# Path pass of a four-layer graph kernel: another order of gathers and scatters on GpSimd

## The reference, cut to what matters

```
f0 = x0 @ W_l10 * na * INV_SQRT_MUL            # features of every node
f1 = einsum('num,uv->nvm', x1, W_l11) * na3 * INV_SQRT_MUL
h  = silu(edge_len_emb @ W_mlp1 / 4);  w = h @ W_mlp2 / 8      # weights of every edge
g0, g1 = f0[i], f1[i]                          # gather at the edge's source
m0a = w0 * g0 * sh0
m0b = w3 * (g1 * sh1).sum(-1) * INV_SQRT3
m1a = w1 * g0 * sh1;  m1b = w2 * g1 * sh0
n   = segment_sum([m0a, m0b, m1a, m1b], j) / sqrt(16)          # sum at the destination
out = ...n @ W_l2...;  alpha = (n0a @ A0 + n0b @ A1) * na * INV_SQRT_2MUL
x   = layernorm(x + sc + alpha * out)
```

## Time and profile before

| what | us |
|---|---|
| median of three timed executions | 5012.12 (5004.49 to 5012.53) |
| the profiled execution's own time | 5035.27 |
| its span, first to last instruction | 5033.5 |
| path pass on POOL, first gather to end of last scatter | 4471.9 to 5025.0 |
| POOL busy over the span | 2801.2 (56%) |
| PE, DVE, ACT busy over the span | 3759.1, 3757.5, 3210.8 |

### The profile page before, as it was taken

How to read it: one execution, slowest core, us unless ns; L and a number is a source line. 1 busy time by engine, 2 the same in 40 slices (tenths; PEclk the granted TensorE clock), 3 DMA queues, 4 the chain that set the end, 5 groups by cost and what they waited for, 6 DMA issues and landing times. The chain is left out here.

```text
span 5033.5 us, 104447 instructions
## 1 busy us (share of the span) xinstructions
PE 3759.1 (75%) x23663; PEld 3111.3 (62%) x23663; DVE 3757.5 (75%) x10843; ACT 3210.8 (64%) x11475; POOL 2801.2 (56%) x2759
## 2 busy tenths in 40 slices
PE   6355889966786677767776878878698997967775
PEld 5254778855556554745575555556587886856664
DVE  1576789978878886978696877879687786747665
ACT  2022779967887686868685543358698795646554
POOL 0473767711760375047302767767476776757776
PEclk9699999978998798979876767779899998978777
DMA  8899999955885597568665446657599896862221
GB/s 180 111 289 284 358 371 317 284 151 157 265 271 153 164 295 247 148 193 278 226 181 150 151 150 184 202 171 240 192 344 327 293 354 223 246 140 61 64 69 52
DMA packets 918273, 1074.23 MB, mean 213 GB/s; under 512 B 202779, under 2 KB 565065, under 8 KB 917106
## 3 DMA queue, kind: packets, MB, share of 16 engines
q1 hardware_dynamic: 763570, 890.24, 54.1%
q0 software_dynamic: 90944, 180.06, 14.1%
q10 hardware_dynamic: 63556, 1.81, 1.8%
HBM read 509.54 MB, written 566.14 MB: 214 GB/s over the span
## 5 line engine op out<-in xcount | busy, mean ns | idle before, releaser
L2366 POOL DMA_INDIRECT H<-gat_rows,src_i x784 | 801.1, 1022 | 876.0 <-POOLq L80 638.0
L1917 POOL DMA_INDIRECT s_G<-sage_rows,src_i x588 | 595.3, 1012 | 286.4 <-issue 175.9
L1696 POOL DMA_INDIRECT r_G<-rel_rows,idx x392 | 404.6, 1032 | 165.9 <-issue 116.7
L2555 PE MATMUL p_M<-Wg,p_hT 128*128 128x132 f32 x2352 | 342.3, 290 | 59.3 <-DVE p_res L2612 45.3
L2555 PEld LDWEIGHTS p_M<-Wg,p_hT 128*128 128x128 f32 x2352 | 296.8, 196 | 106.6 <-issue 91.4
L2612 DVE SCALAR_TENSOR_TENSOR p_res<-p_M,p_rr,cg 128x132 f32<-128x132 f32 x1176 | 333.8, 346 | 2.7 <-PE p_M L2555 1.7
L2694 PEld LDWEIGHTS p_pl_p<-Wn,p_pl_h 128*128 128x128 f32 x1568 | 204.1, 197 | 205.4 <-ACT p_pl_h L2788 158.5
L1305 PE MATMUL d_S<-ones,d_sqT 128*128 128x1 f32 x1568 | 227.6, 266 | 135.6 <-DVE d_ve L1450 135.6
L1709 PE MATMUL r_t<-r_oh,relv 8*128 8x512 f32 x294 | 203.9, 779 | 166.1 <-DMA r_G<-rel_rows,idx 79.0
L2694 PE MATMUL p_pl_p<-Wn,p_pl_h 128*128 128x128 f32 x1568 | 223.3, 287 | 136.2 <-ACT p_pl_h L2788 136.2
L1305 PEld LDWEIGHTS d_S<-ones,d_sqT 128*128 128x128 f32 x1568 | 221.9, 218 | 162.4 <-issue 128.9
(11 more groups left out here) (483 smaller groups left out, 12423.8 us busy)
## 6 DMA issues: line engine op xcount, KB each, us to landing
gat_rows<-p_res SPq DMA_DIRECT2D x294, 264.0 KB
sage_rows<-p_pl_s SPq DMA_DIRECT2D x294, 256.0 KB
gat_rows<-x_row SPq DMA_DIRECT2D x98, 536.0 KB
gat_rows<-d_res SPq DMA_DIRECT2D x147, 264.0 KB
d_hs<-gat_rows SPq DMA_DIRECT2D x147, 256.0 KB
s_hT<-sage_slots_t SPq DMA_DIRECT2D x147, 256.0 KB
slot_rows<-H SPq DMA_DIRECT2D x49, 544.0 KB, 11.4
x_x<-in_x SPq DMA_DIRECT2D x98, 256.0 KB
```

Source lines behind the costliest of these rows:

```text
L1696: pool.indirect_dma_start(self.G[:, g % 4, k, :], None, table, bass.IndirectOffsetOnAxis(index[:, c:c + 1], 0), bounds_check=bound, oob_is ...
L1917: pool.indirect_dma_start(self.G[:, g % 4, k, :], None, kn.st[self.l], bass.IndirectOffsetOnAxis(kn.idx[:, c:c + 1], 0), bounds_check=boun ...
L2366: pool.indirect_dma_start(kn.H[:, c, 0:width], None, table, bass.IndirectOffsetOnAxis(index[:, c:c + 1], 0), bounds_check=bound, oob_is_er ...
L2555: mm = pe.matmul(self.pM[self.bank(b, j)][:, k // 2, (k % 2) * TW:(k % 2 + 1) * TW], self.hT[l][:, b.s2, k * P:(k + 1) * P], kn.Wg[:, l, : ...
```

## The change: what it does

It replaces the fixed distance of 12 groups by a formula. After the gathers of group g, all scatter groups up to `due` are issued, where `due = max(g + 1 - 15, 0) * 41 // 34`. Scatter groups are issued in the same order as before and with the same waits; gathers too. Written out, scatter group 0 follows the gathers of group 15, then one scatter group follows each gather group, except that two follow those of groups 19, 24, 29, 34, 39, 44 and 48, and eight are left for the end.

```
-        LATE = 12
+        FIRST, LAST = 15, 8
...
+        put = 0
         for g in range(kn.KG):
             if g >= 2:
                 pool.wait_ge(self.gin[(g - 2) % 4], ((g - 2) // 4 + 1) * 16 * KT)
...
-            if g >= LATE:
-                place(g - LATE)
-        for g in range(kn.KG - LATE, kn.KG):
-            place(g)
+            due = max(g + 1 - FIRST, 0) * (kn.KG - LAST) // (kn.KG - FIRST)
+            for n in range(put, due):
+                place(n)
+            put = max(put, due)
+        for n in range(put, kn.KG):
+            place(n)
```

## The result

The changed kernel took 4982.29 us (median of 5 timed executions, 4978.33 to 4990.09) against 5004.49 for the kernel before (5 executions, 5000.35 to 5012.53). The ratio is 0.9955, 95% interval 0.9941 to 0.9969: about 22 us faster. The forecast was 4992 us and, against the starting median of 5012.12, 0.9960. The ratio came as forecast; the absolute time is 9.7 us under the forecast and 0.7 us under the stated range.

The account below looks back on a forecast made before the run. POOL's gathers and scatters bound the path pass, except at six waits for VectorE. 7.4 us at the head, 0 in the middle and 13.7 less some 1 at the end make 20 us off 5012.12: 4992 us, range 4983 to 5007.

Parts of the forecast that it names:

- Level: Whole kernel: 20 us taken off the timed median of 5012.12, itself 23 us under the profiled execution, gives 4992 us.
- 21.1 us is all that any reordering can win: Path pass: POOL's six waits for VectorE, 22.9 us less 0.30 ordinary gap each, cap the gain at 21.1 us.
- Head: Start of path pass: three more gather groups before scatter 0 remove POOL's 7.72 us wait, winning 7.4 us.
- Middle: Middle of path pass: compute keeps up with a scatter group every 9.9 us instead of 10.9; term zero.
- 1 us of cover at the tightest: Middle, after a doubled scatter: results come at T + 26.0 at worst, wanted at T + 27.
- End: End of path pass: compute is 22 us ahead, so 13.7 us of POOL waits go, less some 1 us.
- 1 to 4 given as a sign: Path pass: POOL's wait for VectorE falls from 22.9 us to 1 to 4, all ahead of scatters 42 to 44.
- (a): Last steps: TensorE at low clock, a 12.17 us step between norms 42 and 43; 15 us won, 4997; chance 0.19.
- (b): Path pass: longer POOL instructions, stops at doubles and end waits leave 9 us won, 5003, nothing measurable; chance 0.17.
- (c): Middle: compute becomes the bound, period rises over 9.9 us and the kernel is slower, 5028 at 10.8; chance 0.06.
- about 7.3 us of work: Middle: compute's period of 10.9 us held 3.6 us of waiting, leaving about 7.3 us of work per group.
- (d): Head: sixteen gather groups come first instead of fifteen; the sum is the same, no chance of its own.

Follow-up runs that it names:

- the edit to the dots: Changed kernel's VectorE reduction of the dots written as two additions; POOL durations 420.4 to 407.7 us, from e_pick_act to e_both.
- the head's half alone: Against the changed kernel, sixteen gather groups first but one scatter group behind each, no doubled scatters; ratio 1.0006 to the kernel before, pass 564.5 us.
- e_far: Against the changed kernel, twenty-five gather groups go ahead of the first scatter instead of sixteen, same end; ratio 0.9957 to the kernel before, pass 537.7 us.
- e_pick_act: Changed kernel with the copy of the edge records moved from VectorE to ScalarE; ratio 0.9951 to the kernel before, pass 542.6 us.
- e_both: Changed kernel with the record copy on ScalarE and the dots' reduction as two additions; ratio 0.9933 to the kernel before, pass 530.7 us.
- e_two_adds: Changed kernel with only the dots' reduction written as two VectorE additions; ratio 0.9932 to the kernel before, pass 533.4 us.

## Why the prediction was right in its steps and wrong in its time

- **Level, the step that failed: "The timed median of 5012.12 is 23 us under that execution; taken off it, 20 us give 4992 us".** That median was the middle of three executions. With two more it was 5004.49, and over the jobs of this study the same kernel had medians of 5004.49, 5012.59, 5009.17, 5016.8 and 5011.73; the changed one 4982.29, 4992.75 and 4993.46. Two of the last three are within 1.5 us of 4992. The gain was about right: 22.2, 19.8 and 18.3 us between the medians of the three pairs, against 20. Of the 9.7 us by which the forecast missed, 7.6 are the starting level and 2.1 the gain. The time fell 0.7 us out of the range because its lower end, 5004.49 - 21.1, took the lowest of three executions for the lowest level, and a median of five came out as low. That those five were as low stays without a cause; no trace sets it apart.
- **"21.1 us is all that any reordering can win".** It holds for the waits. As a floor of the time it was wrong in kind (the medians of the first pair differ by 22.2), since POOL's durations differ by 15 us between traces of one kernel (412.9 and 427.6) and by 13 within a job with the edit to the dots (420.4 and 407.7). I had put 0 to +2 us for them; measured for this change: -1.7, -4.2 and +0.6 us in three pairs.
- **Head.** 7.4 us and a first scatter at 85.4 us: 7.42 and 85.25. But the head's half alone gave 0.8, so "7.4 us won" is right only in company with the end, which the forecast did not say.
- **Middle.** Zero was right; no POOL wait stands at a doubled scatter, not even at the period of e_far. The "1 us of cover at the tightest" was too dark a view: up to group 40 no norm of the changed kernel ended less than 8.09 us ahead of its scatter (group 23: 4746.99 and 4755.08). The pair of late steps that the forecast allowed for did not fall there.
- **End.** The last gather ends 478.0 us into the pass (forecast 4950.2 - 4471.9 = 478.3), scatter 44 starts at 508.0 (506.5 to 508.3), POOL ends at 533.8 (532.2 to 534.0). Norm 41 to 42 took 8.35 us and not 6.69, 42 to 43 6.58, at the low end of 6.58 to 8.4; the two errors cancel. The waits left at the end are 3.5 us over the ordinary gap, more than the 1 us of the sum; the view's count of 5.6 us, and the 4.4 us of the three waits in it, are above the 1 to 4 given as a sign, and they stand where it said. The sum of 20 us was measured as 19.4, 21.0 and 17.4 in the pass.
- **Rivals.** (a) did not occur: no step of 12 us between norms 42 and 44. (b) no; its sign "gathers over 1.2 us" could tell nothing, as single gathers of that length stood in the kernel before (1.42 us), and the mean gather stayed at 1.07. (c) is excluded down to a period of 8.9 us. The "about 7.3 us of work" set against it was too low: e_far took 8.6 to 9.0 us a step with few waits. (d) sixteen groups do come first, without effect on the sum.

## What to carry to other kernels

When one in-order queue serves both ends of a pipeline with few buffers at its end, as here, its order sets the compute's pace: give the last stage more than its share early, so that the compute is ahead when the first stage's work runs out. Taking a wait away at the head alone moves it to the end. And before a time is forecast to a few parts in a thousand, the spread of the starting median has to go into both ends of the range; compare a stage by its own start and end, since here 30 of 50 us between two traces lay ahead of the code that had changed.

## What the runs showed of the hardware that I had not expected

One and the same indirect DMA instruction on GpSimd took 0.97 to 2.3 us, and the sum over one pass of 392 differs by 15 us between traces of one kernel. It is long only beside VectorE: no such instruction that overlapped none of VectorE's multiplications and additions on two SBUF inputs took over 1.07 us in any of the 16 traces, and those that overlapped them for 0.6 us or more (the norm apart) took 1.13 to 1.37 us on average. Rewriting one VectorE reduction as two additions brought 67 long ones down to 29 (e_pick_act to e_both). The box of the Trainium skill (SBUF — State Buffer, section "SBUF: two separate sides") names a copy in fp32 from SBUF to SBUF as what locks GpSimd out. With that copy moved to ScalarE, 39 of the long ones stood where they had stood, so here it is not what makes most of them long (there the measurement decides); whether it adds a little is open, as one trace each of e_two_adds and e_both, 2.9 us of durations apart, cannot tell.
